# A last normalization stage moved into the experts' block, with its rows split between ScalarE and POOL

## The reference, cut to what matters

```
h = _L0_tok_ref(x, tok_W, tok_b, class_token, pos_emb)          # 64 x 197 x 192
h = _layernorm(h + _L0_attn_ref(h, ...))
h = _layernorm(h + _L0_ffn_ref(h, Wg, W1, W2))                  # experts, two per token

def _layernorm(x, axis=-1, eps=1e-05):
    m = jnp.mean(x, axis=axis, keepdims=True)
    v = jnp.var(x, axis=axis, keepdims=True)
    return (x - m) / jnp.sqrt(v + eps)
```

## Time and profile before

| | us |
|---|---|
| median of 3 runs | 2377.52 |
| lowest and highest of them | 2372.65, 2378.88 |
| the profiled execution, its own time | 2373.45 |
| its span, first to last instruction | 2371.7 |
| attention, to the barrier behind it | up to 1366.8 |
| experts, to the barrier behind it | 1366.8 to 2303.1 |
| last stage | 2303.1 to 2371.7 |

### The profile page before, as it was taken

The page is one execution under the profiler, slowest core; times in us unless marked ns, Lnnn a source line. Parts: engine busy times, 40 slices in busy tenths (PEclk is TensorE's granted clock), DMA queues, the critical chain, the costliest instruction groups (busy, mean ns, idle before and its releaser), DMA issues. The chain is left out here.

```text
span 2371.7 us, 49114 instructions
## 1 busy us (share of the span) xinstructions
PE 2143.0 (90%) x14772; PEld 2075.0 (87%) x14772; DVE 1591.5 (67%) x4304; ACT 1096.8 (46%) x2873; POOL 1561.6 (66%) x2294
## 2 busy tenths in 40 slices
PE   4999999999999999999999369999999999999950
PEld 4898998999999999999998369999999999999950
DVE  4577776877777777777767346666666666666646
ACT  2444444444444444444444135454544545454537
POOL 3356665767676767666665557777777777777743
PEclk9999999999999999999999679999999999999985
DMA  5657777776676656565643143201010110001338
GB/s 155 155 116 130 130 129 128 133 138 136 137 136 135 144 129 141 131 142 129 142 98 75 31 119 58 42 3 26 2 28 3 28 23 6 2 2 26 62 69 287
DMA packets 231952, 219.70 MB, mean 93 GB/s; under 512 B 90963, under 2 KB 212050, under 8 KB 230800
## 3 DMA queue, kind: packets, MB, share of 16 engines
q1 hardware_dynamic: 134512, 146.55, 25.6%
q10 hardware_dynamic: 43040, 56.78, 12.3%
q0 software_dynamic: 54272, 14.76, 5.0%
HBM read 152.91 MB, written 95.25 MB: 105 GB/s over the span
## 5 line engine op out<-in xcount | busy, mean ns | idle before, releaser
L1104 POOL DMA_INDIRECT x_tokens<-yout,e_entry x240 | 381.4, 1589 | 180.5 <-DVE yout L1251 134.2
L651 PE MATMUL Y<-p,vp 128*102 128x198 f32 x1536 | 362.1, 345 | 17.3 <-ACT ysb L482 12.0
L443 POOL DMA_INDIRECT expert_lists<-entry,slot x256 | 289.0, 1129 | 54.3 <-issue 54.3
L1266 DVE TENSOR_TENSOR a<-UP,gate 128x384 f32<-128x384 f32 x320 | 178.4, 558 | 217.7 <-ACT gate L1218 212.4
L487 ACT ACTIVATE p<-ST 128x396 f32<-128x396 f32 x384 | 191.4, 499 | 264.7 <-PE ST L623 254.8
L1173 PE MATMUL Y<-w,a_hi 128*128 128x384 f32 x960 | 304.4, 354 | 2.0 <-DVE a_lo L1256 2.0
L1084 POOL DMA_INDIRECT rows<-x_wide,e_entry x240 | 249.6, 1040 | 77.0 <-issue 72.1
L1218 ACT ACTIVATE gate<-GT 128x384 f32<-128x384 f32 x320 | 157.6, 492 | 295.9 <-PE UP L1160 295.9
L141 POOL TENSOR_TENSOR word_p<-word_p 1x1 f32<-1x1 f32 x416 | 86.5, 208 | 306.0 <-ACT p L489 297.2
L409 POOL TENSOR_TENSOR x_lo<-x,x_hi 128x396 fp32r<-128x396 f32 x192 | 208.0, 1085 | 89.3 <-ACT x_hi L465 87.4
L651 PEld LDWEIGHTS Y<-p,vp 128*102 128x102 f32 x1536 | 222.8, 171 | 32.1 <-issue 12.0
(11 more groups left out here) (182 smaller groups left out, 6326.7 us busy)
## 6 DMA issues: line engine op xcount, KB each, us to landing
x<-in_xt ACTq DMA_DIRECT2D x180, 198.0 KB, 4.8
q<-qk_features SPq DMA_DIRECT2D x384, 74.2 KB
k<-qk_features SPq DMA_DIRECT2D x192, 148.5 KB
qk_features<-qk_hi SPq DMA_DIRECT2D x96, 198.0 KB
qk_features<-qk_lo SPq DMA_DIRECT2D x96, 198.0 KB
e_raw<-in_wexp SPq DMA_DIRECT2D x8, 1408.0 KB, 6.3
rb<-rd ACTq DMA_DIRECT2D x128, 74.2 KB
t_x<-x_tokens SPq DMA_DIRECT2D x16, 576.0 KB, 5.1
```

The lines of the kernel that those rows point to most:

```text
L443: pool.indirect_dma_start(d["lists"][:, :], bass.IndirectOffsetOnAxis(ap=slot[o][0:REAL[t], t, c:c + 1], axis=0), entry[o][0:REAL[t], t, c ...
L651: return pe.matmul(Y[0:VW1, 0:TI], v0, p32[b][:, hh, 0:TI], start=start, stop=stop)
L1104: pool.indirect_dma_start(d["x1"][:, :], row_of(cc, t), yout[q][:], None, bounds_check=N - 1, oob_is_err=False, compute_op=ALU.add)\
L1266: dve.tensor_tensor(a32[m % 2][:], UP[m % 2][:, 0:TILE3], gate[m % 2][:], ALU.mult)\
```

## The change

`last_block` is gone; its work stands at the end of `expert_block`, inside the same block, so the barrier between the two is gone too. SP starts the loads once all `s_out` have counted the last scatters.

The 12608 rows are cut otherwise: groups of 2, 4, fifteen times 6, and 2 row tiles of 128 rows, and a last one of 64 rows, 19 groups in all. There are six buffers (`LB`) instead of four. Of a group of `t` row tiles ACT writes the first `t - t // 3` and POOL the last `t // 3`: four and two of six, three and one of four, and all by ACT in the groups of two and one.

The order on the engines: POOL does the power of group c and then its row tiles of group c-1. ACT does its row tiles of group c and then issues the store of group c-1, once ACT's and POOL's parts of c-1 are complete. DVE keeps its order, without the helper words. SP loads group c once ACT and POOL have finished group c-6. All loops of the stage are written out.

```diff
-def expert_block(nc, d):
+def expert_block(nc, d, out):
+    LB, LT = 6, 6
+    last_tiles, at = [], 0
+    for t in [2, 4] + [LT] * 15 + [2]:
+        last_tiles.append((at, P, t))
+        at += P * t
+    last_tiles.append((at, N - at, 1))
+    NL = len(last_tiles)
...
+        def last_rows(ap, c):
+            at, rows, t = last_tiles[c]
+            return ap[at:at + rows * t, :].rearrange("(p t) c -> p t c", t=t)
+        def by_pool(c):
+            return last_tiles[c][2] // 3
+        def pool_tiles(c):
+            return sum(1 for n in range(c + 1) if by_pool(n))
+        def last_mean(dve, c):
+            q, (_, r, t) = c % LB, last_tiles[c]
+            dve.wait_ge(s_rstd, c + 1)
+            dve.scalar_tensor_tensor(out=last_shift[q][0:r, 0:t], in0=last_mv[q][0:r, 0:t, 0], scalar=-1.0,
+                                     in1=last_rstd[q][0:r, 0:t], op0=ALU.mult, op1=ALU.mult).then_inc(s_shift, 1)
+        def last_store(act, c):
+            q, (_, r, t) = c % LB, last_tiles[c]
+            act.wait_ge(s_oa, c + 1)
+            wait(act, s_op, pool_tiles(c))
+            act.dma_start(last_rows(out, c), last_o[q][0:r, 0:t, :]).then_inc(s_st[q], 16)
...
         def _(sp):
...
+            for q in range(6):
+                sp.wait_ge(s_out[q], 16 * (NCH // 2))
+            for c in range(NL):
+                q, (_, r, t) = c % LB, last_tiles[c]
+                if c >= LB:
+                    sp.wait_ge(s_oa, c - LB + 1)
+                    wait(sp, s_op, pool_tiles(c - LB))
+                sp.dma_start(last_x[q][0:r, 0:t, :], last_rows(d["x1"], c)).then_inc(s_in[q], 16)
...
         def _(pool):
             for n in range(2):
                 pool.memset(rows[n][:], 0.0).then_inc(s_zero, 1)
+            pool.memset(last_half[:], -0.5).then_inc(s_half, 1)
...
             for q in range(6):
                 pool.wait_ge(s_out[q], 16 * (NCH // 2))
+            def last_part(c):
+                q, (_, r, t) = c % LB, last_tiles[c]
+                if by_pool(c):
+                    pool.wait_ge(s_shift, c + 1)
+                    wait(pool, s_st[q], 16 * (c // LB))
+                    for n in range(t - by_pool(c), t):
+                        ins = pool.tensor_scalar(last_o[q][0:r, n, :], last_x[q][0:r, n, :],
+                                                 last_rstd[q][0:r, n:n + 1], last_shift[q][0:r, n:n + 1],
+                                                 ALU.mult, ALU.add)
+                    ins.then_inc(s_op, 1)
+            pool.wait_ge(s_half, 1)
+            for c in range(NL):
+                q, (_, r, t) = c % LB, last_tiles[c]
+                pool.wait_ge(s_var, c + 1)
+                pool.tensor_tensor(last_rstd[q][0:r, 0:t], last_var[q][0:r, 0:t], last_half[0:r, 0:t],
+                                   ALU.pow).then_inc(s_rstd, 1)
+                if c:
+                    pool.wait_ge(s_rstd, c)
+                    last_part(c - 1)
+            pool.wait_ge(s_rstd, NL)
+            last_part(NL - 1)
...
         def _(act):
...
+            for c in range(NL):
+                q, (_, r, t) = c % LB, last_tiles[c]
+                wait(act, s_st[q], 16 * (c // LB))
+                act.wait_ge(s_shift, c + 1)
+                act.wait_ge(s_rstd, c + 1)
+                for n in range(t - by_pool(c)):
+                    ins = act.activation(last_o[q][0:r, n, :], last_x[q][0:r, n, :], ACT.Identity,
+                                         bias=last_shift[q][0:r, n:n + 1], scale=last_rstd[q][0:r, n:n + 1])
+                ins.then_inc(s_oa, 1)
+                if c:
+                    last_store(act, c - 1)
+            last_store(act, NL - 1)
+            for q in range(LB):
+                act.wait_ge(s_st[q], 16 * len(range(q, NL, LB)))
...
         def _(dve):
...
+            for c in range(NL):
+                q, (_, r, t) = c % LB, last_tiles[c]
+                dve.wait_ge(s_in[q], 16 * (c // LB + 1))
                 for n in range(t):
-                    ins = dve.bn_stats(stats[q][0:rows, n, :], a[q][0:rows, n, :])
+                    ins = dve.bn_stats(last_stats[q][0:r, n, :], last_x[q][0:r, n, :])
                 ins.then_inc(s_stat, 1)
...
+                if c:
+                    last_mean(dve, c - 1)
+                dve.wait_ge(s_stat, c + 1)
                 for n in range(t):
-                    ins = dve.bn_aggr(mv[q][0:rows, n, :], stats[q][0:rows, n, :])
+                    ins = dve.bn_aggr(last_mv[q][0:r, n, :], last_stats[q][0:r, n, :])
                 ins.then_inc(s_mv, 1)
                 dve.wait_ge(s_mv, c + 1)
-                dve.tensor_scalar(var[q][0:rows, 0:t], mv[q][0:rows, 0:t, 1], EPS, None, ALU.add)\
+                dve.tensor_scalar(last_var[q][0:r, 0:t], last_mv[q][0:r, 0:t, 1], EPS, None, ALU.add)\
                     .then_inc(s_var, 1)
...
+            last_mean(dve, NL - 1)
...
-    expert_block(nc, d)
-    last_block(nc, d, out)
+    expert_block(nc, d, out)
```

More of the change, by code:

```diff
@@ L981, in expert_block @@
     W1C = 2 * 2 * HID
+    LB, LT = 6, 6
[4 more added lines that the diff above has]
+    last_tiles.append((at, N - at, 1))
+    assert 0 < N - at <= P
+    NL = len(last_tiles)
     with ExitStack() as ctx:
@@ L1044, in parts @@
             return src.rearrange("p (m c) -> p m c", c=C), w2[e][:, to, 0, :], w2[e][:, to, 1, :]
+        last_x, last_o = ([sb(f"t_{name}_{n}", [P, LT, C], F32) for n in range(LB)] for name in ("x", "o"))
+        last_stats = [sb(f"t_stats{n}", [P, LT, 6], F32) for n in range(LB)]
+        last_mv = [sb(f"t_mv{n}", [P, LT, 2], F32) for n in range(LB)]
+        last_var, last_rstd, last_shift = ([sb(f"t_{name}_{n}", [P, LT], F32) for n in range(LB)]
+                                           for name in ("var", "rstd", "shift"))
+        last_half = sb("t_half", [P, LT], F32)
+        s_in = [sem(f"t_loaded{n}") for n in range(LB)]
+        s_half = sem("t_half_ready")
+        s_stat, s_mv, s_var, s_rstd = sem("t_stats"), sem("t_mean"), sem("t_variance"), sem("t_rstd")
+        s_shift, s_oa, s_op = sem("t_shift"), sem("t_out_by_scalar"), sem("t_out_by_pool")
+        s_st = [sem(f"t_stored{n}") for n in range(LB)]
+        def last_rows(ap, c):
[15 more added lines that the diff above has]
+            act.dma_start(last_rows(out, c), last_o[q][0:r, 0:t, :]).then_inc(s_st[q], 16)
         block = ctx.enter_context(nc.Block())
@@ L1278, in _ @@
                 y_out(NCH - 1, t)
[L1281 to L1368, removed]
@@ L1376, in body @@
-                words.wait((s_stat, c + 1), (s_o, c - (NB - 1)))
+                if c:
+                    last_mean(dve, c - 1)
+                dve.wait_ge(s_stat, c + 1)
                 for n in range(t):
-                    ins = dve.bn_aggr(mv[q][0:rows, n, :], stats[q][0:rows, n, :])
+                    ins = dve.bn_aggr(last_mv[q][0:r, n, :], last_stats[q][0:r, n, :])
                 ins.then_inc(s_mv, 1)
                 dve.wait_ge(s_mv, c + 1)
-                dve.tensor_scalar(var[q][0:rows, 0:t], mv[q][0:rows, 0:t, 1], EPS, None, ALU.add)\
+                dve.tensor_scalar(last_var[q][0:r, 0:t], last_mv[q][0:r, 0:t, 1], EPS, None, ALU.add)\
@@ L1382, in body @@
                     .then_inc(s_var, 1)
-            chunks(dve, body)
-            turned_mean(NCH, 0, RP, RT)
-        @block.scalar
-        def _(act):
-            def body(c, turn, q, rows, t):
-                wait(act, s_st[q], turn * 16)
-                act.wait_ge(s_shift, c + 1)
-                for n in range(t):
-                    ins = act.activation(o[q][0:rows, n, :], a[q][0:rows, n, :], ACT.Identity,
-                                         bias=shift[q][0:rows, n:n + 1], scale=rstd[q][0:rows, n:n + 1])
-                ins.then_inc(s_o, 1)
-                act.wait_ge(s_o, c + 1)
-                dst = out_v[c] if rows == P else rest(out, 0)
-                act.dma_start(dst, o[q][0:rows, 0:t, :]).then_inc(s_st[q], 16)
-            chunks(act, body)
-            for q in range(NB):
-                act.wait_ge(s_st[q], (NCH // NB + (q == 0)) * 16)
+            last_mean(dve, NL - 1)
```

2 lines of the change are left out of this document (removed).

## The result

The changed kernel takes 2357.63 us (median of 8 runs, 2352.51 to 2365.24) against 2381.39 us for the kernel before (8 runs, 2372.65 to 2388.12). The ratio is 0.9914, with a 95% interval of 0.9895 to 0.9934: faster by 0.9%. The profiled execution took 2355.76, its span is 2354.0 us, so again some 1.8 us lie around the span.

The account below looks back on a forecast made before the run. It took DMA as the last stage's middle bound, with ACT close by: 54.4 us transfer plus 6.8 idle from 2296.85 ends at 2358.1, gain 13.3 us, giving 2360.1 for the profiled execution and 2362 forecast, range 2353 to 2370.

Parts of the forecast that it names:

- Two of my own signs of being wrong: Last stage: wrong if mixed rate leaves 341 to 372 GB/s, or late stores open DMA holes behind 2310.
- The barrier, 6.3 us: Before the last stage: without POOL's drain between, SP's first load goes out at 2296.85 instead of 2303.16, gain 6.3 us.
- POOL's drain: Before the first load: 5.81 us, taken as no work (2.4 us kept otherwise); at the end, 1.6 us behind the stores.
- 54.4 us of transfer at 356 GB/s: Last stage: 9.68 MB in and 9.68 MB out keep all 16 DMA engines busy 54.4 us, unchanged by the edit.
- DMA has more in it: Last stage, rival: share 0.97 may fill itself, packets waiting for one another; gain 19.3 us, to 2356; chance 0.15.
- 6.8 us of DMA idle time: Last stage after the change: start 1, hole behind first loads 1, middle 1.3, tail 3.5, in us.
- Middle: ACT's relief hidden behind DMA: Middle of last stage: ACT and DVE 2.4 us a group, POOL 2.5, DMA 3.3, so DMA is the bound.
- The later store, taken as a cost: Last stage's opening: store 0 waits for ACT's group 1, going out at 2305.7; DMA hole put at 1 us (0 to 3).
- Six buffers, taken as 30 row tiles ahead instead of 24: Last stage's opening: six buffers take 30 row tiles, 2.95 MB or 8.1 us of loads, where four took 24.
- POOL's row tile, 0.5 us (0.3 to 1.09): Last stage: time of POOL's row-tile instruction, not yet seen on POOL, two per group, giving POOL 2.5 us a group.
- slower rival: Last stage: POOL's 31 row tiles set the pace, 0.3% slower than before from 1.6 us per row tile; chance 0.03.
- What had to show: Trace signs: first load about 2296.9, ACT off the chain, two POOL instructions per group, DMA share 0.95 or more from 2307.

Follow-up runs that it names:

- own store: Changed kernel with all row tiles by ACT and each store issued directly behind its own group, not one group later: 67.0 us to ACT's closing branch.
- even groups: Changed kernel with the earlier cut into 16 groups of six row tiles and one of 64 partitions x 5: 58.4 us to ACT's branch, 60.7 to the end.
- the early drain: Changed kernel plus one POOL drain right behind its wait for the last scatters: stage 57.8 us to the end, 57.4 to ACT's branch.
- the last one: Changed kernel with all row tiles by ACT and no POOL drain at the end of either block: 2354.32 us, ratio 0.9904 to the kernel before.

## Why the prediction was right, point by point

The time (2362 against 2357.63, range 2353 to 2370) and the sign were right. The way there was in good part not, and so the hit is partly luck: of the terms of the sum, some were wrong, and two of them against each other. The forecast gain of 13.3 us compares with 17.7 between the two spans and 23.8 between the medians, and 2357.63 lies nearer to the 2356 of a rival than to 2362. Two of my own signs of being wrong came true: the mixed rate left 341 to 372 GB/s, and DMA had a hole up to 2312. From the first load's issue to ACT's closing branch I had 61.2 us; it was 2350.9 - 2297.9 = 53.0.

- *The barrier, 6.3 us.* Right: the first load went out 3.57 us after the scatter, forecast 3.51. The blocks merged alone gave 7.3.
- *POOL's drain.* Taken as no work of POOL's: right, the first power wasn't held up. That it would come again at the end was said, with 1.6 us behind the stores; it was 2.9 (ACT's branch at 2350.9, POOL's semaphore at 2353.8), and 3.1 to the end of the span. It should have stood in the sum, which ended with the stores.
- *54.4 us of transfer at 356 GB/s.* The step that failed, and by most. 19.36 MB at 420 are 46.1 us, 8.3 less. I had read the share of 0.97 as DMA being full. It is no measure of that: with four buffers a share of 0.96 to 0.99 goes with 339 to 353 GB/s, with six and the later store 0.98 went with 324 for 4 us (the first stretch shown for ACT alone) and 1.03 with 419 to 421 for 20 and more, and with six and the own store 1.00 with 367. The rival *DMA has more in it*, with a chance of 0.15, was the true one in its mechanism, and the 388 GB/s of the weight loads was its row. The page of the Trainium skill, DMA: Bandwidth & Descriptors, "Where 436 GB/s comes from", names some 358 GB/s for HBM and 435 for the fabric. The 421 of pure copying between DRAM and SBUF lies well above the first and near the second, so here, with one core at work, the first was no bound.
- *6.8 us of DMA idle time.* Right in sum: 53.0 - 46.1 = 6.9. In parts the hole was larger (from 2309 to 2312 some 0.8 MB of what 420 GB/s would carry are missing, 1.9 us; forecast 1). In the last 7 us the rate was 300 GB/s, which makes the tail's loss some 2 us by the same reckoning, where 3.5 were forecast.
- *Middle: ACT's relief hidden behind DMA.* The conclusion was right, and sharper than I gave it: with ACT alone the stage took 56.9 us to its branch against 56.6, no difference that can be told. The reason was incomplete. I kept 0.6 us around the store in ACT's group; but with the store one group later they vanish, so that ACT alone needs 2.63 us a group, less than DMA's 2.8.
- *The later store, taken as a cost.* It does cost at the two ends, as worked out. In the middle it is one of the two edits that carry the gain. I had read ACT's idle 0.6 us in the chain and not asked what it was.
- *Six buffers, taken as 30 row tiles ahead instead of 24.* Mis-sized: they are worth 10 us, in the middle. Own store with four buffers is 70.7 with even groups, an estimated 69 with small ones by the 1.8 above (that kernel was not run); own store with six is 67.0, later store with four 66.6, both together 56.9. So each edit alone gives some 2 to 4 us, together they give 12 to 14. Before, ACT's 3.4 us a group and the round trip of four buffers (346 GB/s with the later store, which is 3.4 us a group too) stood level, and behind both DMA was at 2.8.
- *POOL's row tile, 0.5 us (0.3 to 1.09).* 510 ns. The slower rival needed 1.6.
- *Loop and helper words at nothing.* At most some 1.1 us, by the merged kernel, and not shown to be theirs.
- *What had to show.* The start (SP's first load 0.1 us behind POOL's wait), the two instructions per group, ACT off the chain and the DVE waits did. The DMA share of 0.95 from 2307 on did not, as it was 0.75 from 2309 to 2312, and the rate left the band of 341 to 372 upward.

In one line: 13.3 forecast, + 8.1, nearly all because the transfer ran at up to 420 GB/s, - 2.7 for the drain behind the stores, makes the 18.7 us that the stage gained. The drain and 1.0 us lost elsewhere left 4.4 us between this profiled execution's 2355.76 and the 2360.1 that the sum gave for it.

## What to carry to other kernels

A DMA share near 1 doesn't show that DMA is the bound; compare the rate with what a plain copy of the same shapes reaches, which costs one run. Where a stage has two bounds level, such as an engine's group and the round trip of a buffer, an edit to one shows little: test them as a pair before dropping either. An engine that issues its own stores should do so one group late, if there are buffers enough for it: with four it gave little here, with six 10 us. Where semaphores already wait for POOL's indirect DMAs, as here, a barrier behind them can be made without its drain, or the drain put where POOL waits anyway. In the stage that was worth 2.7 to 5.8 us; a shorter device time than the changed kernel's was not shown for it.

## What was unexpected in the hardware

A drain of POOL took 5.80 to 5.83 us behind the experts' gathers and scatters, whether 480 or 736 of them stood before it, even 50 us after the last had landed (2.76 behind attention, with 256). Where POOL's last instruction still runs as the drain begins, the row is longer by as much: 7.04 us in the kernel before without the first drain, 6.99 with even groups. A second drain without such DMAs in between took 0.05 us. What it does in that time no run here shows.

TensorE's granted clock made the experts' part differ by 3 us. At each of the seven changes of expert TensorE waits 2.03 us, and behind some of these waits the clock falls from its upper level (2.4 GHz) to the lower one (1.2 GHz) for some 3.5 us: in the kernel before behind one of the seven, in the changed kernel behind three. The two more make the 3.5 us by which its experts' part is longer. Two equal stretches of 20 us around one such change, the changed kernel and then the kernel before (columns as in the earlier trace rows):

```profile
1944.30:1964.30 20.00, 17.97 (x104) 17.72 (x103) 10.38 (x21) 8.01 (x19) 11.76 (x10) 0.91 0.23 74
```

```profile
1946.80:1966.80 20.00, 17.97 (x115) 17.71 (x114) 11.54 (x24) 9.46 (x22) 12.99 (x12) 1.00 0.23 74
```

In the same time TensorE did 104 matmuls in the one and 115 in the other, and its granted clock was 0.91 and 1.00 on the mean. The experts' part, from the barrier to the last scatter, took 926.2 to 926.8 us in eight of the kernels profiled and 928.9 to 930.0 in six: the changed kernel, the ones without closing drain, with four buffers and rows shared, with even groups, without the drain behind attention, and the last one. Five of the six share rows with POOL, but the last doesn't, and the one with the early drain shares them and had 926.4. So what decides it stays open; the code of TensorE is the same in all.
